# Four-direction scan stage: decay and drive kept by rows and by columns, an image's chunks unrolled, merges on half the array

## What is computed

```python
def _s6(x, ...):                    # x: the pixels in one order
    u = _linear(x, xw, xb)
    bc = _linear(x, bcw, bcb)
    delta = _linear(x, dw, db)
    Bm, Cm = jnp.split(bc, 2, axis=-1)
    A_bar = jnp.exp(-jax.nn.softplus(delta))
    B_bar = (1.0 - A_bar) * Bm
    elems = (A_bar, B_bar * u)      # decay, drive
    _, h = jax.lax.associative_scan(combine, elems, axis=1)   # h = A_bar*h + B_bar*u
    return _linear(Cm * h, yw, yb)
s1 = x.transpose(0, 2, 3, 1)...     # by rows
s2 = x.transpose(0, 3, 2, 1)...     # by columns
s3, s4 = s1[:, ::-1], s2[:, ::-1]   # both backwards
y_cat = jnp.concatenate([y1, y2, y3, y4], axis=-1)
y_merged = _linear(y_cat, mw, mb)
gate = jax.nn.sigmoid(_linear(y_cat, gw, gb))
out = _linear(y_merged * gate, ow, ob)
```

## Time and profile before

| what | us |
|---|---|
| three runs | 4073.1, 4078.38, 4082.28 (median 4078.38) |
| the profiled execution | 4069.57, span 4067.7 |
| four-scan phase: first slot's matmul, first scan, last gate | 2604.4, 2647.3, 3289.7 |
| busy over the span | TensorE 3375.5, DVE 2700.0, ACT 2799.4, POOL 1643.9 |

### The profile page before, as it was taken

One profiled execution on the slowest core, in us unless ns is written; L12 is line 12 of the kernel. 1 busy time (PEld: TensorE's weight loads), 2 busy tenths in 40 slices (PEclk: granted clock), 3 DMA queues, 4 the chain that ended last, 5 costly groups with the idle time before them and its releaser, 6 DMA issues. The chain is left out here.

```text
span 4067.7 us, 72899 instructions
## 1 busy us (share of the span) xinstructions
PE 3375.5 (83%) x20680; PEld 1903.7 (47%) x20680; DVE 2700.0 (66%) x4346; ACT 2799.4 (69%) x5115; POOL 1643.9 (40%) x1502
## 2 busy tenths in 40 slices
PE   5799999978679899999996668699999868677756
PEld 2688888833234344444442224344444324466622
DVE  2566666667059999999999927466666657322256
ACT  4455555568789889898895439577777659566656
POOL 0233333300258889898897610055555510000000
PEclk9899999989889999999999979899999989889989
DMA  4000000012474665757655122100000012400022
GB/s 94 25 14 14 15 14 15 13 49 53 132 193 129 183 189 150 203 142 201 181 148 141 52 70 59 33 16 15 15 15 15 10 32 59 91 17 13 13 55 52
DMA packets 209772, 297.72 MB, mean 73 GB/s; under 512 B 74150, under 2 KB 194134, under 8 KB 209242
## 3 DMA queue, kind: packets, MB, share of 16 engines
q1 hardware_dynamic: 198826, 285.75, 26.9%
q10 hardware_dynamic: 10800, 10.34, 1.1%
HBM read 193.87 MB, written 102.03 MB: 73 GB/s over the span
## 5 line engine op out<-in xcount | busy, mean ns | idle before, releaser
L1586 POOL TENSOR_TENSOR mam_hc<-mam_h,mam_cs 128x896 f32<-128x896 f32 x336 | 703.8, 2095 | 183.8 <-DVE mam_h L1551 86.0
L1551 DVE TENSOR_TENSOR_SCAN mam_h<-mam_a,mam_kept,mam_dbx 128x448 f32<-128x448 f32 x672 | 738.0, 1128 | 23.5 <-ACT mam_a L1437 22.2
L1318 PE MATMUL mam_ps_y<-mam_hc,mam_ident 128*128 128x448 f32 x1344 | 573.3, 560 | 130.6 <-POOL mam_hc L1586 130.4
L1972 POOL TENSOR_TENSOR scan_ch<-scan_h,scan_cs 128x392 f32<-128x392 f32 x256 | 347.4, 1374 | 554.8 <-DVE scan_h L1938 554.8
L1437 ACT ACTIVATE mam_a<-mam_ft,mam_a_neg 128x448 f32<-128x448 f32 x672 | 409.3, 657 | 79.5 <-DVE mam_h L1551 78.6
L1318 PEld LDWEIGHTS mam_ps_y<-mam_hc,mam_ident 128*128 128x128 f32 x1344 | 250.1, 193 | 431.5 <-POOL mam_hc L1586 219.8
L1538 DVE TENSOR_TENSOR mam_dbx<-mam_ps_u,mam_bs 128x448 f32<-128x448 f32 x672 | 381.3, 611 | 32.3 <-DMA mam_bs<-dram_bc 32.3
L766 POOL TENSOR_TENSOR att_prob<-att_prob,att_share 128x588 f32<-128x588 f32 x128 | 151.8, 1186 | 451.6 <-DVE att_share L951 451.6
L1938 DVE TENSOR_TENSOR_SCAN scan_h<-scan_turned_in,scan_start 128x392 f32<-128x392 f32 x192 | 252.8, 1335 | 27.3 <-ACT scan_turned_in L1857 26.0
L1812 PE MATMUL scan_ps_merged<-scan_ch,scan_w_merge 128*128 128x392 f32 x512 | 231.3, 534 | 45.3 <-POOL scan_ch L1972 43.1
L2092 PE MATMUL lstm_ps<-lstm_hs,lstm_w_h 64*128 64x224 f32 x1344 | 171.1, 409 | 97.9 <-DVE lstm_hs L2175 97.9
(11 more groups left out here) (215 smaller groups left out, 7643.4 us busy)
## 6 DMA issues: line engine op xcount, KB each, us to landing
mam_taps<-normed SPq DMA_DIRECT2D x1008, 43.5 KB
mam_bs<-dram_bc SPq DMA_DIRECT2D x28, 896.0 KB, 14.4
mam_cs<-dram_bc SPq DMA_DIRECT2D x28, 896.0 KB, 16.3
mam_ft<-dram_steps SPq DMA_DIRECT2D x42, 448.0 KB, 4.7
normed<-f_staged SPq DMA_DIRECT2D x384, 38.1 KB
f_mixed<-mixed SPq DMA_DIRECT2D x384, 36.8 KB
dram_gs<-mam_gs SPq DMA_DIRECT2D x56, 224.0 KB, 2.3
mam_gt<-dram_gs SPq DMA_DIRECT2D x56, 224.0 KB, 2.7
```

Source lines behind the costliest of these rows:

```text
L1318: mm = pe.matmul(ps_y[p % 2][:, 0:MT], ident[:], hc[t % 2][:, i, :], start=False, stop=(t % 8 == 7 and i == 1))
L1551: dve.tensor_tensor_scan(h[:, n % 8, :], a[t % 3][:, i, :], dbx[:, i, 0:MT], kept[:, at:at + 1], ALU.mult, ALU.add).then_inc(scanned, 1)
L1586: pool.tensor_tensor(hc[t % 2][:], h[:, row:row + 2, :], cs[:, 2 * pair:2 * pair + 2, :], ALU.mult).then_inc(weighed, 1)
L1972: pool.tensor_tensor(out, hd, in_order(cs, 1 - half, d, t, p), ALU.mult).then_inc(weighed, 1)
```

## The change

Only `four_scan_phase` and its weights change.

1. Decay and drive are kept twice, by rows and by columns (`by_column`, as large as the rings). ACT writes the column copies: of decay as a second sigmoid straight out of `ps_in`, of drive by one copy per front chunk (`turn`). All four scans read the rings in place; the six copies into `turned_in` go.
2. The biases of the projections go into the matmul: a row of ones in `xin` (four small DMAs ahead of the loads) and a row of `w_in`. The activation `us` goes: DVE multiplies `ps_in[U]` by `rest` (`share`), and `ps_in[B]` by that (`drive_with`).
3. The scans start from the last column of the other `h` buffer, or from a zero; the `start` instruction goes.
4. Merges: per direction two matmuls of 64 partitions x 128 columns, one per image, each into its own bank, both halves (merged, gate) in one matmul. The gate's sigmoid and the product are then two instructions of 64 partitions each.
5. `rest`, `ub`, `ch`, `gate`, `prod`, `result` have one buffer. POOL waits for the merges of the chunk before, not of the one before that.
6. New orders in a slot (ACT, DVE, and the projections DELTA, U, C, B, each with a wait of its own), and the 8 slots of a stage are unrolled.

```diff
-        w_merge = buf.sbuf("w_merge", [P, 2, DIRS, P])
+        w_merge = buf.sbuf("w_merge", [P, DIRS, P])
...
-        turned_in = [buf.sbuf(f"turned_in{p}", [P, DIRS - 1, 2, N]) for p in range(2)]
+        by_column = {name: buf.sbuf(f"{name}_by_column", [P, 2 * PIXELS])
+                     for name in ("decay", "drive")}
         h = [buf.sbuf(f"h{p}", [P, DIRS, N]) for p in range(2)]
-        start = [buf.sbuf(f"start{p}", [P, DIRS]) for p in range(2)]
-        ch = [buf.sbuf(f"ch{p}", [P, DIRS, N]) for p in range(2)]
-        gate = [buf.sbuf(f"gate{p}", [P, N]) for p in range(2)]
-        prod = [buf.sbuf(f"prod{p}", [P, N]) for p in range(2)]
-        result = [buf.sbuf(f"result{p}", [LAT, N]) for p in range(2)]
+        zero = buf.sbuf("zero", [P, 1])
+        ch = buf.sbuf("ch", [P, DIRS, N])
+        gate = buf.sbuf("gate", [P, N])
+        prod = buf.sbuf("prod", [P, N])
+        result = buf.sbuf("result", [LAT, N])
...
-        ps_merged = buf.psum("ps_merged", [P, BANK])
-        ps_gate = buf.psum("ps_gate", [P, BANK])
+        ps_merged = [buf.psum(f"ps_merged{image}", [P, BANK]) for image in range(2)]
...
-                peeled = b is not None and isinstance(b, int) and b == 0
-                if peeled:
-                    for p in range(2):
-                        slot(f, b, half, 0, p, p == 1)
-                with eng.Fori(0, K // 2 - int(peeled)) as t:
-                    for p in range(2):
-                        slot(f, b, half, t + int(peeled), p, b is not None)
+                first = b is not None and isinstance(b, int) and b == 0
+                for k in range(K):
+                    slot(f, b, half, k, k % 2, b is not None and not (first and k == 0))
...
+        def scan_order(name, half, d, k):
+            at = k if d in FORWARD else K - 1 - k
+            tile = {"decay": decay, "drive": drive}[name] if d in BY_ROW else by_column[name]
+            return ring(tile, half)[:, at * N:(at + 1) * N]
+
+        def turned_rows(name, half, k):
+            return ring(by_column[name], half).rearrange("p (x y) -> p y x", y=SIDE)[
+                :, k * ROWS:(k + 1) * ROWS, :]
...
+                for p in range(2):
+                    for image in range(2):
+                        row = 32 * image + C
+                        sp.dma_start(xin[p][row:row + 1], w["ss_ones"]
+                                     ).then_inc(weights_in, 16)
...
-                        pe.wait_ge(sided, done(c - 1, 4))
-                        pe.wait_ge(multiplied, done(c - 1))
-                        for i in range(4):
+                        c = f * K + k
+                        pe.wait_ge(loaded[p], f * (K * 16) + (k // 2 * 32 + 32))
+                        for i, read, count in (
+                                (DELTA, sided, done(c - 1, 4) - 1), (U, multiplied, done(c - 1)),
+                                (C_, sided, done(c - 1, 4)), (B_, fronted, done(c - 1))):
+                            pe.wait_ge(read, count)
...
-                        for a, ps in enumerate((ps_merged, ps_gate)):
-                            mm = pe.matmul(ps[:, 0:N], w_merge[:, a, n, :], ch[p][:, n, :],
+                        for rows, ps in zip((IMAGE_0, IMAGE_1), ps_merged):
+                            mm = pe.matmul(ps[:, 0:N], w_merge[rows, n, :], ch[rows, n, :],
...
-                    act.wait_ge(gated, done(c - 2))
-                    act.activation(gate[p][:], ps_gate[:, 0:N], ACT.Sigmoid,
-                                   bias=merge_b[:, 1:2]).then_inc(sigmoided, 1)
-
-                def store(c, p, earlier):
+                    act.wait_ge(gated, done(c - 1))
+                    act.activation(gate[IMAGE_0], ps_merged[0][IMAGE_1, 0:N], ACT.Sigmoid,
+                                   bias=merge_b[IMAGE_1, 1:2])
+                    act.activation(gate[IMAGE_1], ps_merged[1][IMAGE_0, 0:N], ACT.Sigmoid,
+                                   bias=merge_b[IMAGE_0, 1:2]).then_inc(sigmoided, 1)
...
+                def turn(c, half, k):
+
+                    act.wait_ge(fronted, done(c))
+                    act.activation(turned_rows("drive", half, k),
+                                   ring(drive, half)[:, k * N:(k + 1) * N].rearrange(
+                                       "p (y x) -> p y x", x=SIDE), ACT.Copy).then_inc(turned, 1)
+
+                def slot(f, b, half, k, p, has_tail):
+                    if f is not None and k > 0:
+                        turn(f * K + k - 1, half, k - 1)
+                    elif b is not None and k == 0:
+                        turn(b * K + (K - 1), 1 - half, K - 1)
...
-                        for n in range(1, DIRS):
-                            for i, tile in enumerate((decay, drive)):
-                                dst = turned_in[p][:, n - 1, i, :]
-                                if ORDER[n] not in BY_ROW:
-                                    dst = dst.rearrange("p (x y) -> p x y", y=SIDE)
-                                act.activation(dst, in_order(tile, 1 - half, ORDER[n], t, p),
-                                               ACT.Copy).then_inc(turned, 1)
...
+                        act.wait_ge(multiplied, done(c - 1))
                         act.wait_ge(projected, done(c - 1, 4) + 1)
-                        act.activation(us[p][:], ps_in[U][:, 0:N], ACT.Identity,
-                                       bias=biases[:, U:U + 1]).then_inc(sided, 1)
-                        act.wait_ge(projected, done(c - 1, 4) + 2)
                         act.activation(ring(decay, half)[:, at], ps_in[DELTA][:, 0:N],
-                                       ACT.Sigmoid, bias=minus_db[:, 0:1], scale=-1.0
+                                       ACT.Sigmoid, scale=-1.0).then_inc(sided, 1)
+                        act.activation(turned_rows("decay", half, k),
+                                       ps_in[DELTA][:, 0:N].rearrange("p (y x) -> p y x", x=SIDE),
+                                       ACT.Sigmoid, scale=-1.0).then_inc(sided, 1)
+                        act.activation(rest[:], ps_in[DELTA][:, 0:N], ACT.Sigmoid
                                        ).then_inc(sided, 1)
-                        act.activation(rest[p][:], ps_in[DELTA][:, 0:N], ACT.Sigmoid,
-                                       bias=biases[:, DELTA:DELTA + 1]).then_inc(sided, 1)
-                        act.wait_ge(projected, done(c, 4))
-                        act.activation(ring(cs, half)[:, at], ps_in[C_][:, 0:N], ACT.Identity,
-                                       bias=biases[:, C_:C_ + 1]).then_inc(sided, 1)
+                        act.wait_ge(projected, done(c - 1, 4) + 3)
+                        act.activation(ring(cs, half)[:, at], ps_in[C_][:, 0:N], ACT.Copy
+                                       ).then_inc(sided, 1)
+                    if has_tail:
+                        store(b * K + k - 1, 1 - p)
...
+                    dve.wait_ge(outed, done(c - 1))
+                    dve.scalar_tensor_tensor(prod[IMAGE_0], ps_merged[0][IMAGE_0, 0:N],
+                                             merge_b[IMAGE_0, 0:1], gate[IMAGE_0], ALU.add,
+                                             ALU.mult)
+                    dve.scalar_tensor_tensor(prod[IMAGE_1], ps_merged[1][IMAGE_1, 0:N],
+                                             merge_b[IMAGE_1, 0:1], gate[IMAGE_1], ALU.add,
+                                             ALU.mult).then_inc(gated, 1)
+
+                def scan(c, half, k, p, n):
+                    d = ORDER[n]
+                    a, v = scan_order("decay", half, d, k), scan_order("drive", half, d, k)
+                    out, before = h[p][:, n, :], zero[:]
+                    if d not in FORWARD:
+                        a, v, out = a[:, ::-1], v[:, ::-1], out[:, ::-1]
+                    if k > 0:
+                        last = N - 1 if d in FORWARD else 0
+                        before = h[1 - p][:, n, last:last + 1]
+                    dve.tensor_tensor_scan(out, a, v, before, ALU.mult, ALU.add
+                                           ).then_inc(scanned, 1)
+
+                def share(f, k, p):
+                    c = f * K + k
+                    dve.wait_ge(sided, done(c - 1, 4) + 3)
+                    dve.wait_ge(projected, done(c - 1, 4) + 2)
+                    dve.tensor_tensor(ub[:], ps_in[U][:, 0:N], rest[:], ALU.mult
+                                      ).then_inc(multiplied, 1)
+
+                def drive_with(f, half, k, p):
+                    c = f * K + k
+                    dve.wait_ge(multiplied, done(c))
+                    dve.wait_ge(projected, done(c, 4))
+                    dve.tensor_tensor(ring(drive, half)[:, k * N:(k + 1) * N],
+                                      ps_in[B_][:, 0:N], ub[:], ALU.mult
+                                      ).then_inc(fronted, 1)
...
+                        for n in range(3):
+                            if n == 2:
```

(25 more changed lines are left out.)

130 lines of the change are left out of this document (44 added, 86 removed).

## The result

| | median us (lowest to highest, runs) | ratio to before, 95% interval |
|---|---|---|
| before | 4075.74 (4067.93 to 4082.28, 4) | |
| after | 3918.67 (3912.36 to 3920.61, 4) | 0.9613 (0.9591 to 0.9634) |

The change makes the kernel 3.9% faster. The profiled execution took 3912.36 us (span 3910.5), 157.2 less than the one of before; the sum had said 151.

What follows compares the result with a forecast made beforehand. A ring of ACT and DVE waiting on each other was taken as the bound, leaving DVE at 7.8 us a slot afterwards. Gains of 126, 7 and 21 less 3 make 151 us: 3918.6, median about 3927, range 3862 to 3998.

Steps and rivals of the forecast that it cites:

- The sum: Whole kernel: 126 us from 56 slots, plus 7 plus 21 minus 3, gives 151 us saved, median about 3927.
- The slot: Each of the 56 slots of both parts falls from 10.05 to 7.8 us, set by DVE; chance 0.55.
- The loss of the scans to POOL: DVE's scans slowed beside POOL's products: 0.87 us a slot before, scaled by slot length to 1.1 us.
- Rival 1: DVE and POOL take turns in full: 8.6 us a slot, 45 us given back, total 3972; chance 0.13.
- Rival 3: DVE and POOL miss each other: DVE has 6.7 us a slot, 62 us more gained, total 3865; chance 0.11.
- rival 4: ACT's writes by column are slow: at 3.5 us each a slot has 11.5, total 4176; chance 0.04.
- rival 2: Half merges on TensorE don't run together: 8.9 us a slot, some 70 us given back in two stretches, total 3997; chance 0.12.
- The ring of the gate: Slot of both parts: last merge through gates, activations, last scan, product and merge takes 7.3 us, hidden by DVE's 7.8.
- Front alone: The 8 slots with only the front: 4.85 us falls to 4.0 each, a gain of 7 us.
- Start: Phase start: four DMAs of ones behind DVE's clears, 0.58 us each, hold everything up; 3 us lost.
- Back alone: The 8 slots with only the back: 9.95 us falls to 7.3 each, a gain of 21 us.
- Rival 5: TensorE's granted clock falls: at 0.91 still covered, at half speed throughout 13 us a slot, slower; chance 0.03.

Runs made afterwards that it cites:

- run 2: Changed kernel with the four scans reading their drive from a PSUM bank of zeros, POOL's products left as they are: 3866.72 us, ratio 0.9485.
- run 1: Changed kernel with POOL writing ones into ch instead of multiplying state by C, so it hardly reads SBUF: 3849.11 us, ratio 0.9436.
- run 10: Changed kernel with DVE's two products of merged and gate put before the third scan instead of behind it: 3940.95 us, ratio 0.9668.
- run 6: Changed kernel with the result and its two DMAs stored directly behind the gate, ahead of the four front activations: 4246.18 us, ratio 1.0434.
- run 7: Changed kernel with the result stored first, plus four matmuls a slot into an unused PSUM bank where TensorE stood idle: 4175.89 us, ratio 1.0225.

## Why the prediction held, step by step

**The sum: 151 us forecast, 157 measured (median 3918.67, about 3927 forecast), and part of this is luck.** The 56 slots gave 13 us more than forecast, front alone 5 more, the start 3 more; back alone gave 8 less, and 6.7 were lost outside the phase.

**The slot: 7.8 forecast, 7.50 in the steady part, 7.57 in the mean.** The bound was named rightly, and two errors in its size cancelled in part. The loss of the scans to POOL was mis-sized: 1.1 us taken, scaled from the mean, 1.57 measured. Missing from the sum was the overlap of records: most DVE records begin about 0.08 us before the last one's end. The durations of a slot add up to 5.59 (scans) + 2.33 (the rest) = 7.92 us; less 7.50, that is 0.42. The 0.15 for the drive's wait was not needed.

**Rival 1, turns in full, was priced wrongly by its own rule.** The step "the means agree with taking turns, but not over an instruction's whole length" read a mean over scans of which some never met a product: in the trace of before the 192 scans out of `turned_in` take 1.00 us at least, 1.36 in the median and 2.04 at most, so one that met a whole product lost all of it. The ends in the timeline show full turns, with 0.2 us of each record outside them: scans 4 x 0.83, products 2 x 0.8 and 2 x 1.0, so 6.9 us a slot, not 8.6. That floor lies under 7.50 and doesn't bind; when they meet does. Rival 3, that they miss each other, was put at 3865; run 2 made them miss and measured 3867. That the numbers agree is luck, since there the ring (6.76) is the bound, not DVE.

**ACT.** The writes by column take 0.94 and 0.90 us, as taken; rival 4 fell. **TensorE.** 16 half passes take 3.0 us (2.8 taken) and the whole row 6.46 (6.7 taken, run 1), so rival 2 fell. **The ring of the gate** was put at 7.3; run 2, where nothing takes turns, shows 6.76. Its place close under DVE's row was right: runs 10 and 6 put it on top. That the store's move would be worth 327 us, a part of it through the clock, stood nowhere in the prediction, which only said that its DMAs no longer hold up the front.

**Front alone: 7 us forecast, 11.8 measured.** The slot is 3.59 us, not 4.0 (the overlaps again). Before, the last of these slots took 6.01 us and not the 4.85 that I took for all, its projections 4.50 instead of 2.87. And from the first projection to the first product of DVE the way shrank from 6.2 to 4.8 us, with one table load of 1.28 us in it where there were two. **Start: 3 us forecast, 0.2 measured.** The sum had left out that DVE's clear of the block-diagonal `w_merge` goes, 0.91 us ahead of these DMAs. And the four DMAs of ones are issued in 1.12 us together, not at 0.58 each, with TensorE starting 2.2 us behind their issue:

```profile
2595.07 1.12 SPq L1761 DMA_DIRECT2D scan_xin<-in_ss_ones  x4
...
2597.24 1.97 PE L1783 MATMUL scan_ps_in<-scan_merge_t,scan_yw 64*64 64x512 f32 x2 [11.71 <-DMA scan_xin<-in_ss_ones]
```

**Back alone: 21 us forecast, 13.2 measured.** The step that failed is "I take 7.3", for all eight slots. From gate to gate a slot takes 7.9 us in the mean, and the first gate comes 10.9 us behind the first scan (before 10.0), where the sum took a slot of 7.3. Rival 5 asked for a low clock only in the 56 slots. TensorE in two of these slots:

```profile
3091.33 4.79 PE L1819 MATMUL scan_ps_merged<-scan_ch,scan_w_merge 64*128 64x392 f32 x16
3098.71 1.57 PE L1796 MATMUL scan_ps_out<-scan_prod,scan_w_out 128*64 128x392 f32 x2 [2.58 <-DVE scan_prod L1918]
...
3107.37 2.95 PE L1819 MATMUL scan_ps_merged<-scan_ch,scan_w_merge 64*128 64x392 f32 x16
3114.07 0.87 PE L1796 MATMUL scan_ps_out<-scan_prod,scan_w_out 128*64 128x392 f32 x2 [3.76 <-DVE scan_prod L1918]
```

At full clock output follows output after 7.5 us; at the lower one the merges take up to 4.79 us and a slot up to 8.9. The granted clock is 0.84 in this stretch (0.98 before), where TensorE is idle 2.6 to 3.8 us ahead of each output matmul (before 1.4 to 2.5). So the clock explains some 3 of the 8 us that are missing (7.9 less 7.5, seven times); at full clock a slot would still be 7.5, and the first one would still be longer than 7.3. The idleness grew as the merges and copies became shorter. That such idleness lowers the clock is shown by runs 6 and 7 in the stage of both parts; in this stretch it was not tried.
